# Segments of selection, masks in two sets and two-operand one-hot builds in a two-layer graph network

## What is computed

```
gcn(h):  out[d] = sum over edges (s -> d) of (h @ W)[s] * norm(edge)  + self loop + b
L0:      log_softmax(gcn(relu(gcn(h, W1)), W2))
L1:      msg = relu(h[src] + edge_attr @ We + be)
         z = h + segment_sum(msg, dst)
         relu(batchnorm(relu(z @ W1 + b1) @ W2 + b2))
```

## Time and profile before

| | us |
|---|---|
| three runs: median (lowest to highest) | 7237.86 (7178.89 to 7238.14) |
| the profiled execution, its own time | 7202.73 |
| its span in the profile | 7200.9 |
| mean granted TensorE clock | 0.786 of full |

### The profile page before, as it was taken

The page is one execution under the profiler, slowest core; times in us unless marked ns, Lnnn a source line. Parts: engine busy times, 40 slices in busy tenths (PEclk is TensorE's granted clock), DMA queues, the critical chain, the costliest instruction groups (busy, mean ns, idle before and its releaser), DMA issues.

```text
span 7200.9 us, 123340 instructions
## 1 busy us (share of the span) xinstructions
PE 4929.8 (68%) x29893; PEld 3663.6 (51%) x29894; DVE 3687.3 (51%) x11918; ACT 1294.4 (18%) x4290; POOL 3762.4 (52%) x3554
## 2 busy tenths in 40 slices
PE   4566666666666766667666666667777777777777
PEld 4444444444444545555555555555555555555554
DVE  3565666666666554444444444464444444444444
ACT  4211111111111230000000000042222222211113
POOL 2477777777777544444444444454333433344444
PEclk5577777777777667777777777768888888888888
DMA  1122222221222121111111111132222222222223
GB/s 42 46 46 48 46 46 49 46 48 46 46 49 46 48 49 40 40 37 38 42 40 40 37 38 41 42 90 62 55 54 54 56 54 55 55 51 52 51 52 99
DMA packets 239971, 355.98 MB, mean 49 GB/s; under 512 B 68655, under 2 KB 137178, under 8 KB 239545
## 3 DMA queue, kind: packets, MB, share of 16 engines
q0 software_dynamic: 111232, 170.85, 12.8%
q1 hardware_dynamic: 128688, 184.55, 8.1%
HBM read 315.83 MB, written 39.30 MB: 49 GB/s over the span
## 4 chain that ended last, share of the span: by engine, by line
PE 57%; DVE 22%; issue 10%; POOL 4%; DVEq 4%; ACT 2%; DMA 1%; ACTq 0%; POOLq 0%; SPq 0%
PE psum L1202 29%; PE psum L1126 10%; PE psum L1149 8%; DVE rows_g L1594 5%; POOL rows_g L645 4%; DVE x_tab L1587 3%; DVE hot L1553 3%; DVE x_tab L1637 2%; PE psum L1197 2%; DVE hot L1556 2%; PE psum L1134 1%; DVEq L426 1%; PE psum L1070 1%; PE psum L1138 1%; DVE x_tab L1632 1%
## 5 line engine op out<-in xcount | busy, mean ns | idle before, releaser
L645 POOL DMA_INDIRECT rows_g<-table,idx x3476 | 3599.5, 1036 | 3149.1 <-ACT idx L782 2100.9
L1202 PE MATMUL psum<-x_tab 125*128 x12160 | 2080.8, 342 | 607.5 <-DVE rows_g L1594 474.8
L1202 PEld LDWEIGHTS psum<-x_tab 125*128 125x128 bf16 x12160 | 1406.1, 116 | 1258.9 <-issue 645.6
L1564 DVE TENSOR_TENSOR acc<-acc,psum 96x128 f32 x1173 | 328.3, 280 | 2703.9 <-PE psum L1126 2699.7
L1126 PE MATMUL psum<-hot,rows_g 128*96 128x128 f32 x7512 | 1112.1, 300 | 60.0 <-DMA rows_g<-table,idx 43.8
L1126 PEld LDWEIGHTS psum<-hot,rows_g 128*96 128x96 f32 x7512 | 1029.0, 185 | 197.8 <-issue 95.5
L1149 PE MATMUL psum<-x_tab 128*104 128x512 bf16 x2432 | 665.9, 428 | 530.3 <-DVE x_tab L1637 530.3
L780 ACT ACTIVATE attr<-edge 128x12 f32 (+1 forms) x1173 | 243.8, 208 | 3875.0 <-PE psum L1126 3875.0
L1553 DVE TENSOR_SCALAR hot<-iota,attr 128x128 f32<-128x128 f32 x2504 | 694.0, 356 | 81.7 <-issue 38.8
L1149 PEld LDWEIGHTS psum<-x_tab 128*104 128x104 bf16 x2432 | 323.5, 141 | 808.5 <-ACT x_tab L825 322.2
L1587 DVE TENSOR_SCALAR x_tab<-x_tab 125x512 bf16<-125x512 bf16 x3040 | 653.4, 288 | 38.8 <-ACT x_tab L799 38.8
(11 more groups left out here) (251 smaller groups left out, 3441.8 us busy)
## 6 DMA issues: line engine op xcount, KB each, us to landing
x_tab<-sorted_keys SPq DMA_DIRECT2D x304, 250.0 KB
rows_g<-table,idx POOLq DMA_INDIRECT x3476, 2.5
x_more<-in_edge_attr_dram SPq DMA_DIRECT2D x238, 64.0 KB, 1.9
sorted_attr<-x_tab SPq DMA_DIRECT2D x38, 384.0 KB, 3.0
x_more<-sorted_attr SPq DMA_DIRECT2D x152, 96.0 KB
table<-x_tab SPq DMA_DIRECT2D x13, 840.0 KB
x_tab<-in_edge_attr_dram SPq DMA_DIRECT2D x38, 256.0 KB, 2.8
x_tab<-in_x_dram SPq DMA_DIRECT2D x2, 4200.0 KB
```

Source lines behind the costliest of these rows:

```text
L645: pool.indirect_dma_start(out=rows_g[u][0:np_, g * F:(g + 1) * F], out_offset=None, in_=table[p], in_offset=bass.IndirectOffsetOnAxis(ap=i ...
L1202: last = pe.matmul(ps_sel[c], mask[j][:, c * P:(c + 1) * P], tab3[:, bass.ds(w[c] + j, 1), :, :].rearrange("q a k f -> q (a k f)"), start= ...
L1564: dve.tensor_tensor(a, a, ps_agg[t.b], ALU.add).then_inc(fast.added, 1)
```

## The change

- **Segments.** The ten groups of an iteration are cut into four segments, SEGS = (0, 1, 2), (3, 4), (5, 6), (7, 8, 9). In passes 1 and 2 TensorE does for segment i first `select(i)` and then the aggregates of the segment. VectorE does for segment i: the adds of segment i - 1; the masks of selection i + 1 (at the last segment those of the next iteration's first); the one-hot builds HOTS[i]; the join of selection i. The adds of the last segment come at the iteration's end, behind the join of selection 3. The one-hot matrix is built two to four groups ahead.
- **A second set of masks.** Selection i uses set i % 2. `make_masks` waits once, for the whole of the selection before the last one, and then writes ten masks without a wait. The room comes from halving the buffers of edge attributes (EH 6 to 3).
- **Two-operand builds.** `build_hot` is one TENSOR_TENSOR over 128x512 with broadcast operands, and in passes 0 and 1 a second one that multiplies by the weight; `sort_perm` is a TENSOR_TENSOR of 128x2048 against a copy of the ranks repeated 16 times in f16 (`rank_h`, one more instruction in each iteration of pass 0).
- **ScalarE** makes keys two selections ahead and stages by segment. Sorted keys are stored as U16 instead of fp32.
- **Pass 2:** the transposes and edge products of gathered groups stand between the masks' matmuls of a selection (EA_AT: three in the first selection, one in each other).
- The last full iteration is written out behind the loop on VectorE; the test for far edges moves to the end of pass 0; the three bf16 parts of `We` are made by VectorE alone; the table's parts of pass 2 wait for the last join of pass 1.

```diff
+    SEGS = ((0, 1, 2), (3, 4), (5, 6), (7, 8, 9))
-    EH = 6
+    EH = 3
...
-        mask = [at_free.take(GE, BF16)[0:PN, :] for _ in range(KB)]
+        mask_t = [(at_free if k < 14 else at_low2 if k < 16 else at_top2).take(GE, BF16) for k in range(2 * KB)]
+        mask = [[t[0:PN, :] for t in mask_t[k * KB:(k + 1) * KB]] for k in range(2)]
...
             def gin_iter(it):
...
+                for i in range(NP):
+                    key_ahead(2, it, i)
+                    for k in SEGS[i]:
+                        if k in GAT:
+                            gin_copy(Gather(it, GAT.index(k) + LL))
+                        relu_fast(Step(it, k))
+                    stage_seg(2, it, i)
...
                 for j in range(KB):
+                    if p == 2 and j in EA_AT[i]:
+                        g = EA_AT[i][j]
+                        gin_transpose(Gather(it, g + LT))
+                        gin_linear(Gather(it, g + LL))
                     pe.wait_ge(s_mask, 2 * KB + n * KB + j + 1)
                     for c in range(G):
-                        last = pe.matmul(ps_sel[c], mask[j][:, c * P:(c + 1) * P],
+                        last = pe.matmul(ps_sel[c], mask[i % 2][j][:, c * P:(c + 1) * P],
...
             with pe.Fori(0, LOOPS) as it:
-                for k in range(U):
-                    aggregate(1, Step(it, k))
-                    if k in SELECT_AT:
-                        select(1, it, SELECT_AT[k])
+                for i in range(NP):
+                    select(1, it, i)
+                    for k in SEGS[i]:
+                        aggregate(1, Step(it, k))
...
-                for g in range(G):
-                    rel = attr[t.u][0:np_, g:g + 1]
-                    if p < 2:
-                        last = dve.tensor_scalar(hot[t.h][0:np_, g, :], iota[0:np_, 0:W], rel,
-                                                 attr[t.u][0:np_, G + g:G + g + 1], ALU.is_equal, ALU.mult)
-                    else:
-                        last = dve.tensor_scalar(hot[t.h][0:np_, g, :], iota[0:np_, 0:W], rel, None, ALU.is_equal)
+                h = hot[t.h][0:np_, :, :]
+                spread = lambda a: a.unsqueeze(2).to_broadcast([np_, G, W])
+                last = dve.tensor_tensor(h, iota[0:np_, 0:W].unsqueeze(1).to_broadcast([np_, G, W]),
+                                         spread(attr[t.u][0:np_, 0:G]), ALU.is_equal)
+                if p < 2:
+                    last.then_inc(s_hot1, 1)
+                    dve.wait_ge(s_hot1, n + 1)
+                    last = dve.tensor_tensor(h, h, spread(attr[t.u][0:np_, G:2 * G]), ALU.mult)
...
                 n = (p - 1) * RS + it * NP + i
                 dve.wait_ge(s_kb, n + 3)
+                dve.wait_ge(s_sel, KB * (n + 1))
                 for j in range(KB):
-                    dve.wait_ge(s_sel, n * KB + j + 1)
-                    dve.tensor_scalar(mask[j], key_b[i % 2], float(j), None, ALU.is_equal).then_inc(s_mask, 1)
+                    dve.tensor_scalar(mask[i % 2][j], key_b[i % 2], float(j), None, ALU.is_equal).then_inc(s_mask, 1)
...
+                link(it, dve.tensor_copy(rank_h, rank[:, :].unsqueeze(2).to_broadcast([P, SC, 16])))
...
-                dve.tensor_scalar(perm[c % 3], iota_h, rank[:, c:c + 1], None, ALU.is_equal).then_inc(s_perm, 1)
+                split16 = lambda t: t.rearrange("p (a k) -> p a k", k=16)
+                dve.tensor_tensor(split16(perm[c % 3]), split16(iota_h),
+                                  rank_h[:, c, :].unsqueeze(1).to_broadcast([P, SE // 16, 16]), ALU.is_equal).then_inc(s_perm, 1)
...
+            HOTS = ((2, 3, 4), (5, 6, 7), (8, 9), (10, 11))
...
+                    for i in range(NP):
+                        if i:
+                            for k in SEGS[i - 1]:
+                                add_window(p, Step(it, k), at[k])
+                        edge_terms = [Step(it, k) for k in SEGS[i] if p == 2 and k in GAT]
+                        for t in edge_terms[:1]:
                             add_edge_term(fast, t.gi, t.got(2), t.u, EP)
+                        masks_ahead(p, it, i)
...
+                        for k in HOTS[i]:
+                            build_hot(p, Step(it, k))
...
+                        join_rows(p, Step(it, SEL[i]))
+                    for k in SEGS[NP - 1]:
+                        add_window(p, Step(it, k), at[k])
```

177 lines of the change are left out of this document (87 added, 90 removed).

## The result

The changed kernel takes 6833.7 us (median of 4 runs, 6830.3 to 6837.1), the kernel before 7231.4 beside it: ratio 0.9465, 95% interval 0.942 to 0.951. It is faster, by 398 us, where the sum had 982 (7203 to 6221); 6833.7 lies above the range (5960 to 6640). Two of three passes missed their term of the sum.

The account below looks back on a forecast made before the run. It took VectorE's masks, build and join alternating with TensorE's products to bound passes 1 and 2, and a similar ring pass 0, GpSimd nearly full; 7203 + 190 - 716 - 456 = 6221, said as 6220 us, range 5960 to 6640.

Parts of the forecast that it names:

- -716 forecast: Pass 1: period falls from 56.35 to 37.5 us, a gain of 18.85 us times 38.
- the timetable: Pass 1, one iteration worked out by instruction: TensorE waits for VectorE once, about 2 us; ends at 36.9, taken as 37.5.
- the half gain at today's clock (-470): Pass 1 if products keep 7.79 us a selection, half of them at low clock: 44 us an iteration, -470.
- the ring: Pass 0: VectorE's matrices and adds, TensorE's permutes and aggregates wait in turn; step from 4.82 to 5.83 us, +190 in all.
- I take a mean near today's: Pass 0: gathers of 1.16 us plus 0.30 pause, 40 an iteration, need 58.4 us, so GpSimd does not set the period.
- The bound worked out for it (1.5 us in the mean, 72 an iteration, +590): Pass 0: if each of 40 gathers takes 1.5 us in the mean, GpSimd needs 72 us an iteration, +590.
- rival 4: Pass 0 was GpSimd's; if two-operand operations hold up no gather, 226 us go instead of 190 coming: 5805 to 6030; chance 0.10.
- Rival 7: Slower: two-operand chains let no gather in until they end; +700 in pass 0, no gain in passes 1, 2: 7900; chance 0.03.
- The copy is still behind these: Pass 2: copy L867 stands behind ScalarE's sums, so a waiting transpose delays selection 0, which ends at about 16.3 us.
- 44.5 worked out: Pass 2: mean iteration, 45.4 us in the 25 with sums and 42.9 without, taken as 46 for some loss of clock.
- this term: Pass 2: period falls from 58.0 to 46 us, 12.0 x 38 = -456.
- pass 2's of -228: Pass 2, the smaller-gain bound: 52 us an iteration, half the gain, -228.

Follow-up runs that it names:

- the third run of the one-operand matrices: Changed kernel with one-operand permutation matrices in pass 0 and two-operand builds kept, on a chip like the first: 6258.3 us, ratio 0.8635 to the kernel before.
- combined kernel: Changed kernel with one-operand matrices and builds in pass 0, SyncE's keys a selection earlier, ScalarE's copies ahead of its key: 5926.3 and 5917.6 us; slower chip 7178.8.
- the second run of the one-operand matrices: Changed kernel with one-operand permutation matrices in pass 0 and two-operand builds kept, on a slower chip: 7396.7 us, kernel before 7768.

## Why the prediction was wrong

- **Pass 1: right.** -716 forecast, -721 measured, by the timetable: masks off the path, join in time after the first segment. The price of a selection (6.2) came out as 6.4 to 6.5, with the clock at 0.99, and the half gain at today's clock (-470) did not come. That no gain is left without the second set is shown (one set: +22.3 us an iteration, a part of it perhaps by the coarser wait).
- **Pass 0, the ring: right, but not what bounds.** 1.24 a matrix, 5.83 a step; measured 1.215 and 5.84. The step that failed is "I take a mean near today's, 1.16 each with 0.30 of pause: 40 x 1.46 = 58.4, just below the ring's 61". The mean gather is 1.409: 179 of the 1564 last over 3.9 us, none over 2.8 before. From the chain of L1603, which lets a gather in at each operation's end (1.76), I inferred that two-operand operations do so. Those are fp32. The 16-bit two-operand chain keeps a gather that starts beside its first matrix out to its own end and through the build behind it, 4.9 us from the chain's start; the one-operand chain lets such a gather end at 1.56. So it is not only the length (3.5 us for 2.1). Why the two kinds differ no run shows. The bound worked out for it (1.5 us in the mean, 72 an iteration, +590) was near the truth. With one-operand matrices and the two-operand builds left in, the pass takes 54.7 us: without the long matrices the builds cost nothing that can be seen, beside them 4.8 us (on a slower chip).
- **Half of rival 4 was right.** Pass 0 was GpSimd's before as well (40 x (1.089 + 0.30) = 55.6 of 56.4), and it is so in each version on chips like the first. With dearer builds than before the third run of the one-operand matrices is at 54.7, below the kernel before: the ring had slack. What the rival had wrong is the sign of what two-operand operations do to gathers.
- **Rival 7 named the mechanism, the build included, and misplaced its size and reach.** It had gathers starve in every pass; they do so in pass 0 alone, at five chains an iteration, and the mean rose by 0.32, half of the 0.66 from which it would have decided. In passes 1 and 2 the mean gather is 1.02 and 1.00: chains of fp32 builds let them in, and of some 900 gathers in the loops of pass 1 a single one lasts over 1.5 us.
- **Pass 2: the step "The copy is still behind these, and now a transpose that waits for it holds up the products of selection 0 behind it" had the right mechanism and knew one of two causes.** ScalarE's sums hold the copy once an iteration; a late key holds it in every segment. I had read that keys are made two selections ahead and did not follow SyncE's queue, where the key load stands behind the sorted attributes' wait for a join. Without that wait the period is 43.1 to 43.6 us (44.6 to 45.4 in the iterations with sums, 40.5 in the others), against 44.5 worked out (45.4 and 42.9). The late key costs 9.6 to 10 us an iteration, 365 to 380 us, more than the whole miss of this term (7.4 us, 289 in all).
- **Both misses fall on one side** and cost 312 + 289 us, which is the distance from 6221 to 6835 but for 13. The range missed because pass 0's bound of +590 and pass 2's of -228 were each named and never added: with -716 they give 6849.
- The Trainium skill's page "SBUF — State Buffer", section "SBUF: two separate sides", holds the shared ports to be locked for a whole instruction. The trace agrees that GpSimd is held up, and goes further: a gather beside a chain of three instructions of 1.215 us lasted 4.27 us, through the end of each of them. That VectorE would wait in its turn it does not show: 608 matrices took 1.211 to 1.221 us. Nor does it show that the first to start keeps them, as the page has it: the 100 gathers of the kernel before that had started ahead of a one-operand chain still lasted to its end.

## What to carry to other kernels

When VectorE's operations change in kind, ask of each chain without a gap how long it keeps GpSimd's gathers out, and measure it on that kind of operation: here three 16-bit two-operand ones and the build behind them kept a gather out as one whole, while chains of fp32 ones, and mostly those of one-operand ones, let it in sooner; the same count of gathers at +0.32 us each cost more here than the ring that was being watched. When an order is changed on three engines, follow the fourth, the queue that issues the loads: one load that waits for a result stands ahead of the next one's operand, and with a transpose put between a selection's products that lateness reaches the busiest engine. And where two unknown costs have far ends on the same side, add them once before the range is closed.

## What the runs showed of the hardware that I had not expected

- **Chips differ by 8% and more on the same program.** The kernel before took 7231 to 7246 us in the batches of one kind and 7768 to 7833 in the three others. The combined kernel took 5918 to 5926 and 7179, 21% more, so its gain is 18% on the one kind and 8% on the other. Each chip served one batch, so chip and batch cannot be told apart. The traces of the slower batches show TensorE without its next instruction: products that elsewhere run without a gap stand apart, once an iteration at one place of the loop, with "issue" ahead of them. From the second run of the one-operand matrices:

```profile
3727.44 1.48 PE L1216 MATMUL psum<-x_tab,x_more 125*128 x7
3729.26 0.29 PE L1216 MATMUL psum<-x_tab,x_more 125*128 x1 [0.35 <-issue]
3730.00 0.56 PE L1216 MATMUL psum<-x_tab,x_more 125*128 x3 [0.44 <-issue]
3731.37 0.55 PE L1216 MATMUL psum<-x_tab,x_more 125*128 x2 [0.81 <-issue]
3732.79 0.56 PE L1216 MATMUL psum<-x_tab,x_more 125*128 x3 [0.88 <-issue]
```

  24 products take from 3727.4 to 3736.9 there, for 3.9 us elsewhere, and the period of pass 1 is 47.7 us for 37.3, of which these gaps are a part. What keeps the instructions away was not tried.
- **The same gather takes 0.94 to 4.9 us, by where it falls against VectorE's chain.** Counted from the start of a chain of three matrices, the held gathers that start beside the first of them end at 4.90 to 4.92 us with two-operand matrices and builds (189), at 4.30 to 4.31 with one-operand builds (151), and most end at 1.56 with one-operand matrices. Those that start just ahead of a one-operand chain end at 2.19 in 100 cases of the kernel before and in 54 and 79 of the combined kernel, but in none of the third run of the one-operand matrices.
- **Whether two-operand fp32 builds hold gathers less than one-operand ones is not shown.** Beside one-operand matrices the mean gather of pass 0 was 1.05 us with two-operand builds and 1.07 and 1.08 without on one chip. On the three slower ones it was 1.09, 1.09 and 1.10 with them and 1.07, 1.07 and 1.08 without.
- **TensorE's granted clock went with its waits:** 0.79, 0.99 and again 0.79 in pass 1 before, after, and with one set of masks. The mean selection took 7.55, 6.43 and 6.94 us. The products' pace is a part of what a removed wait is worth: 4 x 1.12 = 4.5 of the 19 us that pass 1 gained an iteration, and 2 of the 22.3 us lost with one set.
